# A two-layer graph network on one core: edge counts ahead of edge sums, wider spans, 16-bit one-hots, and a matrix product moved into the edge loop

## What is computed

```python
h0  = relu(layernorm(x))
# layer 0: messages of edges, mean over the edges that end in a node
agg = segment_sum((h0[src] + edge_attr) @ Wm.T + bm, dst) / max(degree, 1)
o   = h0 + gelu(concat(h0, agg) @ Wu.T + bu)
x1  = x + layernorm(o) * gamma + beta
# layer 1: sum over the edges, then two dense layers
h1  = relu(layernorm(x1))
rst = (1 + eps) * h1 + segment_sum(h1[src], dst)
out = x1 + relu(rst @ W1 + b1) @ W2 + b2 + h1
```

## Time and profile before

| | us |
|---|---|
| median of 3 runs (lowest, highest) | 548.49 (548.27, 549.06) |
| the profiled execution | 548.76 |
| its span | 547.0 |
| loop over the groups: first count added to last sum added | 26.79 to 254.3 |
| first `hidden` product | 407.75 |

### The profile page before, as it was taken

How to read it: one execution, slowest core, us unless ns; L and a number is a source line. 1 busy time by engine, 2 the same in 40 slices (tenths; PEclk the granted TensorE clock), 3 DMA queues, 4 the chain that set the end, 5 groups by cost and what they waited for, 6 DMA issues and landing times.

```text
span 547.0 us, 9240 instructions
## 1 busy us (share of the span) xinstructions
PE 473.7 (87%) x3007; PEld 277.5 (51%) x3007; DVE 300.3 (55%) x849; ACT 265.5 (49%) x599; POOL 107.2 (20%) x100
## 2 busy tenths in 40 slices
PE   4399766788898898764989997989999999999997
PEld 3244433344444444333886555658984445844442
DVE  5555998778998888897384699693210000011111
ACT  7755999988888888894501133423002222200000
POOL 1310010110100000110060267334996000000000
PEclk9599999999999999997999998989999999999999
DMA  8985999989999999994060011000000000011110
GB/s 309 364 317 184 371 411 408 332 356 384 377 383 387 389 386 393 384 385 173 1 213 2 19 36 39 19 20 0 1 1 1 0 0 1 0 38 39 39 38 34
DMA packets 31115, 98.93 MB, mean 181 GB/s; under 512 B 3577, under 2 KB 3577, under 8 KB 31067
## 3 DMA queue, kind: packets, MB, share of 16 engines
q1 hardware_dynamic: 30458, 97.27, 47.5%
q10 hardware_dynamic: 608, 1.05, 0.6%
HBM read 95.76 MB, written 2.56 MB: 180 GB/s over the span
## 4 chain that ended last, share of the span: by engine, by line
PE 61%; DVE 16%; ACT 8%; issue 7%; DVEq 3%; SPq 3%; DMA 1%; POOL 1%; POOLq 0%
PE ps L1185 13%; PE ps L1170 12%; PE ps L1058 6%; PE ps L1059 6%; PE ps L973 6%; PE ps L1076 5%; PE ps L942 5%; ACT square L452 4%; DVE A L653 4%; PE ps L915 3%; DVE aggT L662 2%; DVE U L791 2%; PE ps L961 2%; DVEq L638 2%; ACT X L464 1%
## 5 line engine op out<-in xcount | busy, mean ns | idle before, releaser
L653 DVE TENSOR_TENSOR A<-ps,A 128x120 f32 x316 | 89.5, 283 | 46.6 <-PE ps L953 36.3
L452 ACT ACTIVATE square<-iotaF,T_lo 128x128 bf16<-128x128 f32 x316 | 100.9, 392 | 4.1 <-PE ps L953 3.0
L942 PE MATMUL ps<-ea,oneD 128*24 128x256 f32 x1264 | 84.9, 386 | 20.1 <-issue 8.8
L1058 PE MATMUL ps<-AR,Hh 128*128 128x256 f32 (+1 forms) x280 | 92.4, 354 | 7.1 <-ACT AR L514 5.0
L1059 PE MATMUL ps<-AR,Hl 128*128 128x256 f32 (+1 forms) x280 | 87.9, 338 | 0.0
L886 DVE TENSOR_TENSOR U<-ps,U 128x512 f32<-128x512 f32 (+1 forms) x10 | 6.9, 692 | 128.4 <-PE ps L1185 128.4
L1185 PE MATMUL ps<-W2s,hid 128*128 128x512 f32 (+1 forms) x160 | 68.8, 592 | 0.0
L1170 PE MATMUL ps<-aggT,W1s 128*128 (+1 forms) x192 | 67.3, 513 | 0.0
L1058 PEld LDWEIGHTS ps<-AR,Hh 128*128 128x128 f32 x280 | 55.0, 196 | 14.8 <-ACT AR L514 5.3
L942 PEld LDWEIGHTS ps<-ea,oneD 128*24 128x24 f32 x1264 | 32.5, 103 | 54.0 <-issue 24.5
L1059 PEld LDWEIGHTS ps<-AR,Hl 128*128 128x128 f32 x280 | 54.9, 196 | 6.9 <-issue 1.9
(11 more groups left out here) (134 smaller groups left out, 522.3 us busy)
## 6 DMA issues: line engine op xcount, KB each, us to landing
ea<-in_edge_attr_dram SPq DMA_DIRECT2D x78, 1024.0 KB, 8.6
X<-in_x_dram SPq DMA_DIRECT2D x1, 2304.0 KB
xt<-in_x_dram SPq DMA_DIRECT2D x9, 256.0 KB, 2.7
out_dram<-U SPq DMA_DIRECT2D x9, 256.0 KB
W1s<-in_L_gnn_W_dram SPq DMA_DIRECT2D x1, 2048.0 KB, 12.4
W2s<-in_L_gnn_W_dram SPq DMA_DIRECT2D x1, 2048.0 KB, 11.6
WuN<-in_L_gnn_Wu_dram ACTq DMA_DIRECT2D x1, 1024.0 KB, 5.0
WuN<-in_L_gnn_Wu_dram SPq DMA_DIRECT2D x1, 1024.0 KB, 6.5
```

The costliest lines, as they stand in the source:

```text
L452: ins = nc.scalar.activation(square[h][:, j, :], iotaF[:], ACT.Square, bias=idxT["lo"][:, j, n:n + 1], scale=-1.0)
L653: V.tensor_tensor(cols, ps[:, 4 + n % 2, j * KW:(j + 1) * KW].rearrange("p (h w) -> p h w", w=W), cols, ALU.add).then_inc(add_step, 1)
L942: last = T.matmul(ps[rows:rows + WS, n % 2, 0:D // 2].rearrange("p (c d) -> p c d", c=2), oneD[h][:, g * 2 + j, :], data, start=j == 0, st ...
L1058: T.matmul(to, Hh[:, c, rows], AR[:, c, start:start + cols], start=start_bank, stop=False)
```

## The change

- **Counts ahead of sums.** In pass n of the loop the counts of one or two groups are made, 4 groups per 3 passes (`COUNTED`), so all 79 are counted in pass 58 (`FULL`). The sums keep one group per pass.
- **Spans.** Counts and sums use one span, 22 nodes per 256 edges. A group's counts are then added in 2 parts of 220 numbers, where there were 4 of 120; PE accumulates two subtiles in one result. The sums' parts have 88 numbers, before 96.
- **One-hots.** `oneK` has 4 x 220 numbers, made by four instructions from a 16-bit iota with one scalar per partition each, where one instruction made 4 x 120 from a 32-bit iota. Half of `oneS` is made by two such instructions on DVE, and ACT makes the other half.
- **DVE's order.** In a pass: one-hots of the sums, the load of the sums' addresses, then for each group to be counted both adds, the load of the next counts' addresses and six one-hot instructions; then both adds of the sums. The adds of one kind now follow each other.
- **A h0 in the loop.** From pass 60 on (`PIECE_AT`), each pass has one `piece`: 8 products of 512 columns. 19 pieces run in the loop and one after it; ten of 256 columns come later, between the first `map_agg`. ACT converts the counts a piece at a time. The degrees are folded in passes 59 to 65, and the bias is added in passes 67 to 76.
- **Before the loop.** Three of the five weight products and the moments of x move ahead of the loop; POOL zeroes A16; there are 18 preparing steps on DVE instead of 21.
- **Large counts.** If a count is over 4096, what the rounding left is multiplied afterwards as a remainder (`extra`); the second copy of the layers is gone. The branch for groups that span more nodes moves to pass 29.
- **Order of tiles.** The tiles go in plain order, PSUM banks and SBUF places are given out anew, x is loaded earlier, and W1 and W2 later.

```diff
-W = 12
-WS = 24
+W = 22
...
+    COUNTED = [min(NG, (4 * (n + 1) + 2) // 3) for n in range(NG)]
+    COUNTS = [list(range(COUNTED[n - 1] if n else 0, COUNTED[n])) for n in range(NG)]
+    FULL = COUNTED.index(NG)
+    T_AT = [4, 5, 6, 8, 9, 10, 11, 13, 14, 15]
+    U_AT = [7, 12, 16, 21, 26, 32, 37, 42, 47, 52]
+    GEN_AT = 29
+    FOLD_AT = FULL + 1
+    PIECE_AT = FULL + 2
+    PIECES = [(q, c) for q in range(NQ) for c in range(NT)]
...
+            def source_hots(m):
...
+                for j in range(2):
+                    ins = nc.scalar.activation(square[h][:, j, :], iotaF[:], ACT.Square, bias=idxT["lo"][:, 2 + j, m:m + 1], scale=-1.0)
...
+            def counts_hots(m):
+                if m >= HOTS:
+                    dve.wait_ge(counts_done, m - HOTS + 1)
+                for j in range(2):
+                    V.tensor_scalar(oneS[m % HOTS][:, j, :], iotaB[:, 0:P], idxT["lo"][:, j, m:m + 1], None, ALU.is_equal)
+                for j in range(SUB):
+                    last = V.tensor_scalar(oneK[m % HOTS][:, j, :], iotaB[:, 0:KW], idxT["key"][:, j, m:m + 1], None, ALU.is_equal)
+                last.then_inc(hotK_ready, 1)
...
+            def add_counts(m, half, first):
+                cols = A16[:, :, bass.ds(first, W)]
+                if half == 0:
+                    dve.wait_ge(counts_done, m + 1)
+                if m > 0 or half > 0:
+                    dve.wait_ge(add_step, m * 2 + half)
+                V.tensor_tensor(cols, ps[:, 4 + m % 2, half * KW:(half + 1) * KW].rearrange("p (h w) -> p h w", w=W), cols, ALU.add).then_inc(add_step, 1)
...
             for n in range(NG):
-                add_counts(n, 0, first[0])
                 if n + HOTS < NG:
                     sums_hots(n + HOTS)
-                add_counts(n, 1, first[1])
-                if n + HOTS < NG:
-                    counts_hots(n + HOTS)
-                following = offsets(n + 1) if n + 1 < NG else None
-                add_counts(n, 2, first[2])
                 if n > 0:
-                    add_sums_of(n - 1, 0, before[0])
-                add_counts(n, 3, first[3])
+                    sum_first = offsets(n - 1)
+                for m in COUNTS[n]:
+                    for half in range(2):
+                        add_counts(m, half, count_first[half])
+                    if m + 1 < NG:
+                        count_first = offsets(m + 1)
+                    if m + HOTS < NG:
+                        counts_hots(m + HOTS)
...
                 if n > 0:
-                    add_sums_of(n - 1, 1, before[2])
-                before, first = first, following
+                    for half in range(2):
+                        add_sums_of(n - 1, half, sum_first[half])
...
+            def piece(i):
...
+                for f in range(FC):
...
+                    T.matmul(to, Hh[:, c, rows], counted, start=c == 0 and (q < 2 or f % 2 == 0), stop=False)
+                    last = T.matmul(to, Hl[:, c, rows], counted, start=False, stop=c == NT - 1 and (q < 2 or f % 2 == 1))
+                last.then_inc(piece_mm, 1)
...
+                if n >= PIECE_AT:
+                    piece(n - PIECE_AT)
...
+            map_agg(0)
+            map_agg(1)
+            late(0)
+            map_agg(2)
+            late(1)
+            map_agg(3)
+            map_agg(4)
+            pe.wait_ge(agg_done, 2 * FC + 1)
+            for b in range(5):
+                transpose_h1(b)
+                times_A(b, "A")
+                map_agg(b + 5)
```

More of the change, by code:

```diff
@@ L637, in offsets @@
             def offsets(n):
                 _, loaded = nc.values_load_multi_w_load_instructions(
[L639 to L643 removed]
+                    offrow[0:1, n * 4:n * 4 + 2].bitcast(I32), engines=(mybir.EngineType.DVE,), min_val=0, max_val=(NP << 16) - 1,
@@ L1052, in times_A @@
[L1052 to L1059 removed]
+                    to, rows = bank(chunk, f, cols), slice(f * P, (f + 1) * P)
@@ L1158, in _ @@
+            last.then_inc(rst_mm, 1)
+            pe.wait_ge(rst_done, 2)
+            for b in range(NT):
+                last = times_A(b, "E")
+            last.then_inc(rst_mm, 1)
             with pe.If(large > COUNT_MAX):
-                layers(True)
-            with pe.Else():
-                layers(False)
+                pe.wait_ge(rst_done, 4)
+                extra(1)
             pe.wait_ge(w1_in, 16)
```

1092 lines of the change are left out of this document (559 added, 533 removed).

## The result

The changed kernel takes 619.56 us (median of 4 runs, 619.28 to 622.4), the kernel before beside it 548.6. The ratio is 1.130 (95% interval 1.127 to 1.134): 13% slower. I had said slower by 6.8%, 586 us with 526 to 610 as the range. The direction was right and the time was outside the range. The profiled execution took 619.28, its span 617.5.

The account below looks back on a forecast made before the run. Loads bound the loop before, with DVE close below; DVE was to bound the counting passes after. First hidden product at 445 us plus 139.3 gave a 584 us span, forecast 586 us, 6.8% slower, range 526 to 610.

Parts of the forecast that it names:

- those steps are unchanged and PE gives them less cover, so I keep 11: After the loop, first map to first hidden product: 96 us of PE work plus 11 of stalls, 107 in all.
- Dependent adds: DVE's pass: an add waiting for its predecessor starts later, second adds at 0.58 (counts) and 0.41 us (sums).
- Rival 3: DVE's adds: dependent adds are free, 37 us less, 549 us, no change; chance 0.04.
- Address loads: DVE's sequencer: a 0.53 us load, now uncovered, loses 0.36 us per group counted and 0.52 per pass.
- Rival 1: DVE's address loads cost nothing, hidden while DVE is still at work: 530 us, faster; chance 0.20.
- One-hots: DVE's counting passes: six 16-bit one-hots of a group take 0.80 us, 0.26 ns a number.
- Rival 2: DVE's 16-bit one-hots run two numbers a cycle, not four: 1.08 us for six, 608 us; chance 0.17.
- its sign, 0.19 from one-hot to one-hot: Profile after: one-hots of 220 numbers start 0.19 us apart under Rival 2, 0.14 under the forecast.
- where I had allowed 8: Counting phase: 8 us added to 235 for POOL's subtractions, the moved branch, first passes, bias and norm steps.
- the last stretch from the last count add to the first map: Last 19 passes and after: PE's pieces, sums, turns and degrees' products take 64.5 us, 3.2 a pass.
- The general branch and the tail: Branch moved to pass 29 costs 1.5 us; first hidden product to end of span stays 139.3 us.
- the gain that I credited: Stage after the loop shrinks from 153 to 107 us, a gain of 46, while the loop grows by 84.

Follow-up runs that it names:

- maps_first: Changed kernel with `map_agg(b + 5)` given to TensorE ahead of `times_A(b, "A")` after the loop, not behind it: 591.62 us, ratio 1.074.
- before_order: Kernel before with only VectorE's order in a pass changed to that of the change, no instruction added or removed: 611.06 us, ratio 1.112.
- adds_mixed: loads_behind with the adds of the two matrices alternating and the one-hots of the sums moved behind them: 589.25 us, ratio 1.072.
- loads_behind: Changed kernel with the address loads issued behind the six one-hots of a group: 608.10 us, ratio 1.104.
- immediates: Changed kernel with the counts' one-hots comparing with constant 255 instead of a scalar per partition, so all counts are zero: 600.13 us, one run.
- mixed_maps_act3: Changed kernel with the edits of adds_mixed and maps_first, and one of DVE's two `oneS` instructions moved to ACT: 553.99 us, ratio 1.007.
- spread: mixed_maps_act3 with transposes and `u1` spread over passes 4 to 51, `u1` halved from pass 21, h0 added on VectorE in two parts: 544.00 us, ratio 0.991.

## Why the prediction was right in direction and wrong in size

**The step that failed** is "those steps are unchanged and PE gives them less cover, so I keep 11". From the first map to the first hidden product PE has 96 us of work by my count (in maps_first it was busy for 99.9 us between 340 and 452); the stage took 142, which is 46 of stalls and slow clock instead of 11, and 35 us is all of the error in the span (617.5 - 584 = 33.5). I had counted PE's work and carried the stalls of before over, but had not followed the order on PE against the order on DVE. Half of the sentence was right: PE gives less cover. It had to be pursued until it said which instruction waits for which. The diff has it: on PE a map stands behind each product, and DVE's run of steps lies between the two with nothing on PE beside it. That is 3.43 + 4.98 + 1.84 = 10.25 us a round at full clock for 5.27 of work: 5 x 4.98 = 25 us of stalls. The lower clock adds the 14 us worked out above: 39 of the 46. maps_first took 29.4 away by the swap of two lines. What it left of the 39 is DVE's, which then sets rounds of 7.0 us against PE's 5.27: 5 x 1.7 = 9 us. So even without the ring the stage takes 112.6 and not 107, with 16.6 us of stalls and not 11.

**The loop, 336.0 where I had 338.** Here most steps held:

- *Dependent adds.* 0.18 us of idle time before each second add, 79 times for each matrix and 13.9 us of waits for each. Second adds at 0.56 to 0.57 and 0.42, against 0.58 and 0.41. Rival 3 is out. By the Trainium skill ("VectorE: DVE Perf Modes", The DRAIN you can't avoid), which measured eight tensor_copy in a row, a semaphore between chained instructions costs nothing extra; for these short adds the traces here disagree, with 0.47 from add to add in before_order where a free successor follows after 0.19. adds_mixed won 19 us beyond loads_behind by alternating them.
- *Address loads.* The mechanism was right and the size wrong, since I took the length of a load of a whole group (0.53) for that of one value (0.31). In the pass of 3.10 us the first one-hot starts 0.38 after the second add, where a free successor starts after 0.30, and the next count add 0.49 after `oneD`, where 0.16 would do: the loads cost 0.08 and 0.33, where I had 0.36 and 0.52. In before_order, where the load is the long one, DVE is idle for 0.32 ahead of the one-hots. loads_behind won 17.5 us in the passes, not 59. Rival 1, which takes that to its end, is out.
- *One-hots.* 1.08 us for six, not 0.80 (and my sum was short by itself: 1136 x 0.26 ns is 0.30, not 0.26, so 0.84). The slope was right, 0.25 ns a number against 0.26. The Trainium skill ("VectorE: DVE Perf Modes", the perf-mode tier table) puts 16-bit tensor_scalar at four results a cycle and 32-bit at two, and the slopes agree with that ratio: 0.25 here, 0.51 at 32 bits. What was missing is the scalar per partition: immediates shows 0.06 us for it. I had taken the fixed cost, 0.09, from instructions on 10 numbers with a constant; with a scalar per partition it is 0.165 - 128 x 0.00025 = 0.13. Rival 2 named 1.08 exactly, and its sign, 0.19 from one-hot to one-hot, is there, for a reason that is wrong.
- These two errors are of one size and opposite sign: -0.3 for the first load, +0.28 for the one-hots. A pass came out as 3.10 and 5.1 to 5.4 where 3.29 and 5.33 were forecast, and the phase as 238 us where I had 243. The steady passes add up to 39 x 3.10 + 20 x 5.12 = 223 us where I had 235, and what else fell into the phase to 15 where I had allowed 8. That the total is close is luck to that extent.
- *The rest.* The DMA share of 0.76 and 0.71 (0.7 forecast), the first count add at 29.6 (30.3), and the last stretch from the last count add to the first map, 68.3 us (64.5 forecast) with pieces every 3.2 us:

```profile
319.79 1.06 PE L976 MATMUL ps<-ea,oneD 128*22 128x256 f32 x16
...
322.99 1.06 PE L976 MATMUL ps<-ea,oneD 128*22 128x256 f32 x16
```

- *The general branch and the tail* held: the pass with the branch took 6.66 against 5.12 of its like, the 1.5 of the forecast, and from the first hidden product to the end 139.5 (139.3).

**Was the gain that I credited real?** Once the ring is opened the stage from the last sum to the first hidden product is 115 us (maps_first, 337.5 to 452.5) against 153.6 before: 39 of the 46 us. In the change as made the ring took 29 of them back. The credited gain was there and was spent, and the loop's 79.5 us more stood against it from the start.

**Still open.** Against mixed_maps_act3 spread's first 18 passes fell from 67.4 to 60.7 us, and the passes behind them stayed (123.6 and 124.0), so the gain lies where the transposes were thinned out. How much of it comes from that and how much from keeping `u1` whole before pass 21 was not separated. The step down of TensorE's clock was taken away together with the ring, never alone; its 14 us are worked out from the rows.

## What to carry to other kernels

Where a change moves calls of an in-order engine, write for each pair of engines the two orders side by side and look for a ring, an instruction that waits for a result whose maker waits for one queued behind it; one swap here was worth 28 us (619.6 to 591.6). Where one engine is near its bound, the order of its instructions is a resource as large as their number: adds of one matrix in a row and an address load at the wrong place cost 62 us in a kernel that was else unchanged. And put a price on the scalar and the fixed cost before an instruction is split into many short ones.

## What the runs showed of the hardware

- A load of one 32-bit value into a register of DVE's sequencer took 0.31 us, one of two values 0.53. DVE stood idle behind it where no work was queued ahead: 0.32 us in before_order.
- A 16-bit tensor_scalar on VectorE started its successor 0.105 us (128 numbers) and 0.128 us (220) later with a constant, and 0.165 and 0.188 with a scalar per partition.
- 32-bit instructions of DVE on 512 numbers with two inputs from SBUF went from 0.69 and 0.75 us (L840 and L862 in the ring) to 1.78 and 1.76 when GpSimd worked beside them, and GpSimd's own from 1.28 (L390 and L393 in the kernel after, median) to 1.57 and 1.73. One more add on DVE, at 0.61, cost less than the GpSimd instruction that it replaced, at 1.03 of DVE's time.
- With PE idle 5.0 us of every 13 the granted clock was 0.72 to 0.77 on average and products of 512 columns started 0.43 apart; with PE at work 17 of 20 us it was 1.00 and they started 0.23 apart.
